# Every fourth leaky ReLU of the edge scores in two pieces, and the eigenvector parts in the first batches

## The chip, the cores and the metric

One core of a Trainium2 chip runs the whole program. The metric is the device time of one execution in microseconds (us). TensorE (PE in the rows, its weight loads PEld), VectorE (DVE), ScalarE (ACT), GpSimd (POOL) and SyncE (SP) run their own instruction streams and wait for each other on semaphores.

## What is computed

Four graph layers, each `x = layernorm(x + layer(x))`, on x of shape (128 graphs, 64 nodes, 256 features). Layers 0 and 1 (a graph network with windows of an LSTM, a graph convolution with batch norms) lie before the stage of this change. Layer 2 is the edge attention with four heads of 64 features and 512 edges, here cut to its scores:

```python
Xq = (H @ W_lin.T).reshape(bt, n, h, dh)
Qs = Xq[:, src]
Kt = Xq[:, dst]
e = jnp.einsum('behd,hd->beh', jax.nn.leaky_relu(Qs + Kt, 0.2), a)
e = e + jnp.log(A0[src, dst] + EPS)[None, :, None]
# softmax of e over the edges of one source node, then Y = sum of attn * Xv[dst], then Y @ W_out.T
```

Layer 3 needs the eigenvectors U of the normalised Laplacian of the adjacency matrix, and computes `U @ ((relu((U.T @ x) @ W1 + b1)) @ W2 + b2)`.

## The kernel before

The stage is in `edge_attention` (lines 1285 to 1492). The block before it ends with the queries of all graphs in SBUF (`xq`), rows of two graphs on 128 partitions. The stage runs over b = 0 to 127, one graph each, with 128 feature rows in each of C = 2 halves k and E = 512 edges:

- VectorE builds "stacks" (`build(dve, j)`, line 1359): for a batch j of four b it writes the queries of the four graphs as a high part (L1366) and a low part (L1368), four instructions a batch. There are three stacks; from j = 3 on a build waits until the gathers of batch j - 3 are done. Stacks 0 and 1 are built in the block before (`queries_ready`).
- TensorE gathers: for each b two matmuls (L1469) with a stack as weights and the 0/1 matrix `e_gather` as the moving operand give Qs + Kt of all 512 edges in PSUM, `ps_g[b % 3]`, 128x1024, one half k in each of two banks. Gather b waits until the leaky ReLU of b - 3 is done.
- ScalarE runs the leaky ReLU (L1340, Prelu) of both halves at once from `ps_g` into one of seven buffers `leaky`.
- TensorE multiplies with the vector a: `dots(r)` (L1454), eight matmuls for four b, which the profile shows as 16 records. It is issued after the gathers of b = 4r + 6, and waits for the leaky ReLU of 4r + 3.

After each 32 b (a quarter, eight batches) the scores of the quarter go through the softmax: `maximum` (L1381 to L1384), the exponential on ScalarE (L1335, after b % 32 == 12), `total` (L1388 to L1390), `inverse` in two halves (L1394), `weights` (L1397), then four transposes on TensorE (`turn`, L1461, after the gathers of b % 32 == 28), the copy of the high part on ScalarE (L1330, after b % 32 == 31) and the low part on VectorE (L1402). VectorE's order is written out by hand in `on_vector`: in batch j of the next quarter, `maximum` stands behind build j where j % 8 == 2, `total` where it is 4, the halves of `inverse` where it is 5 and 6.

VectorE also computes the eigenvectors for layer 3 in eight parts (`Eigenvectors.part`, lines 388 to 451). `EV_AT` (L1302) says behind which batch each part stands: batches 8 to 27. Part 3 ends with sums of squares, GpSimd makes inverse norms of them (`inverse_norm`, L382 to L386), and part 4 waits for these. The parts work in a part of `xq` whose queries are used up by batch 8 (L1300, `ev.place`). GpSimd's queue holds, behind the norm, six DMAs (L1323) that bring operands of the late values back from DRAM, two as each of three places in `xq` is used up (after stacks 11, 15 and 19). After b = 127 TensorE computes the late values (`LATER`), the last quarter goes through its softmax, and the attention begins; SyncE and GpSimd start its preparation when the last dot products are done.

Of the kernel before, what the change touches and what calls it, by code (L numbers as in the profile page):

```python
# [9 lines left out]
P = 128  # L10
# [479 lines left out]
def overlay(nc, name, shape, dt):  # L490


    with nc.sbuf_tensor(name, shape, dt) as t:
        return t
# [790 lines left out]
def edge_attention(nc, sem, c, m, ev, low, xq, acol, attn, hT, later):  # L1285
# [6 lines left out]
    with ExitStack() as ctx:  # L1292
# [4 lines left out]
        stack = [[sb(f"stack{i}{n}", [P, TWO, D], F32R) for n in range(2)] for i in range(STACKS)]  # L1297
        ps_g = [ctx.enter_context(nc.psum_tensor(f"sc_g{i}", [P, C, E], F32)) for i in range(GATHERS)]
        ps_s = [ctx.enter_context(nc.psum_tensor(f"sc_s{i}", [P, E], F32)) for i in range(2)]
        ev.place(xq[0:N, 6 * E:8 * E])  # L1300
        squares, norms = (sem("ev_" + n) for n in ("squares", "norms"))
        EV_AT = {8: 0, 11: 1, 15: 2, 16: 3, 19: 4, 23: 5, 24: 6, 27: 7}  # L1302
        score, top, tops, ex, run, tot = (xq[:, n * E:(n + 1) * E] for n in range(6))
        load, zero, placed, stacked, gathered, leaked, dotted, diff, exped, weighed, turned, high, low = (
            sem("sc_" + n) for n in ("load", "zero", "placed", "stack", "gathered", "leaky", "dot", "less_maximum",
# [3 lines left out]
        LATER = [GROUPS - 1] + list(range(later.FIRST, GROUPS - 1))  # L1309
        ps_v = [z[:, :, :].rearrange("p c (h d) -> p (c h) d", d=D) for z in ps_g]  # L1310
        BATCH = 2 * TWO
        COLUMN_HALVES = (slice(0, EC // 2), slice(EC // 2, EC))
        def on_sync(sp):
            sp.dma_start(ac[:, :], acol).then_inc(load, 16)
# [10 lines left out]
        def on_scalar(act, weights_ready):  # L1325
            a = nc.scalar

            def weights_hi(q, n=0, part=slice(0, EC)):
                act.wait_ge(turned, q + n + 1)
                a.activation(attn[0][:, part, q * P:(q + 1) * P], ps_s[(q + n) % 2][:, :].rearrange("p (k e) -> p k e", k=EC)[:, part],  # L1330
                             ACT.Copy).then_inc(high, 1)

            def exponent(q):
                act.wait_ge(diff, q + 1)
                a.activation(ex, top, ACT.Exp).then_inc(exped, 1)  # L1335
            for b in range(B):
                act.wait_ge(gathered, b + 1)
                if b >= RING:
                    act.wait_ge(dotted, (b - RING) // 4 + 1)
                a.activation(leaky[b % RING][:, :, :], ps_g[b % GATHERS][:, :, :], ACT.Prelu, alpha=SLOPE).then_inc(leaked, 1)  # L1340
                q, at = b // PER_Q - 1, b % PER_Q
                if q >= 0 and at == 12:
                    exponent(q)
                if q >= 0 and at == PER_Q - 1:
                    weights_hi(q)
            def values(n):
                act.wait_ge(valued, n + 1)
                a.activation(group_of(hT, LATER[n]).rearrange("p c (h d) -> p (c h) d", d=D), ps_v[n % GATHERS], ACT.Copy).then_inc(
                    values_copied, 1)
            values(0)  # L1350
            exponent(QUARTS - 1)
            weights_ready(act)
            values(1)
            values(2)
            for n, part in enumerate(COLUMN_HALVES):
                weights_hi(QUARTS - 1, n, part)
            values(3)

        def build(dve, j):
            if j >= STACKS:  # L1360
                dve.wait_ge(gathered, (j - STACKS + 1) * BATCH)
            for n in range(2):
                h, o = slice(n * N, (n + 1) * N), slice((1 - n) * N, (2 - n) * N)
                rows = xq[h, j * TWO * D:(j + 1) * TWO * D].rearrange("p (t d) -> p t d", d=D)
                hi, lo = stack[j % STACKS][n][h, :, :], stack[j % STACKS][n][o, :, :]
                nc.vector.tensor_copy(hi, rows).then_inc(stacked, 1)  # L1366
                dve.wait_ge(stacked, 4 * j + 2 * n + 1)
                nc.vector.tensor_tensor(lo, rows, hi.bitcast(F32), ALU.subtract).then_inc(stacked, 1)  # L1368
# [72 lines left out]
        def on_tensor(pe):  # L1441
            t = nc.tensor

            def dots(r):
                pe.wait_ge(leaked, 4 * r + 4)
                q, at = r // SLOTS, r % SLOTS
                if r == 0:
                    pe.wait_ge(placed, 2 * C)
                if at == 0 and q >= 2:
                    pe.wait_ge(high, q - 1)  # L1450
                    pe.wait_ge(low, q - 1)
                for k in range(C):
                    for j in range(4):
                        i = t.matmul(ps_s[q % 2][32 * j:32 * j + 32, :], apad[:, k, at * 32:at * 32 + 32], leaky[(4 * r + j) % RING][:, k],  # L1454
                                     start=at == 0 and k == 0, stop=at == SLOTS - 1 and k == C - 1, tile_position=(0, 32 * j))
                i.then_inc(dotted, 1)

            def turn(q, n=0, part=range(EC)):
                pe.wait_ge(weighed, q + n + 1)
                for k in part:  # L1460
                    i = t.transpose(ps_s[(q + n) % 2][:, k * P:(k + 1) * P], tops[:, k * P:(k + 1) * P], c["ident"][:, :])  # L1461
                i.then_inc(turned, 1)
            for b in range(B):
                if b % BATCH == 0:
                    pe.wait_ge(stacked, b + 4)
                if b >= GATHERS:
                    pe.wait_ge(leaked, b - GATHERS + 1)
                for k in range(C):
                    i = t.matmul(ps_g[b % GATHERS][:, k], stack[b // BATCH % STACKS][b % 2][:, b // 2 % TWO, k * P:(k + 1) * P],  # L1469
                                 m["gather"][:, :], start=True, stop=True)  # L1470
                i.then_inc(gathered, 1)
                if b % 4 == 2 and b > 4:
                    dots(b // 4 - 1)
                if b >= PER_Q and b % PER_Q == PER_Q - 4:
                    turn(b // PER_Q - 1)
            dots(B // 4 - 1)
            for n, g in enumerate(LATER):
                if n:
                    pe.wait_ge(rows_in[n - 1], 32)
                if n >= GATHERS:  # L1480
                    pe.wait_ge(values_copied, n - GATHERS + 1)
                hi, lo = later.rows(g)
                for r in range(TILES):
                    f = slice(r * P, (r + 1) * P)
                    for k in range(C):
                        i = product(t, ps_v[n % GATHERS][:, r], (hi[:, k, f], lo[:, k, f]), [z[:, k] for z in later.weights], k == 0, k == C - 1)
                i.then_inc(valued, 1)
            turn(QUARTS - 1, 0, range(EC // 2))
            turn(QUARTS - 1, 1, range(EC // 2, EC))
# [1190 lines left out]
def network(nc, a, out):  # L2680
# [14 lines left out]
    with ctx:  # L2695
# [10 lines left out]
        with ExitStack() as wide:  # L2706
            m, spectral, scores, place, later, hidB, layers = first_layers(nc, layer_sem, wide, c, bi, ev, hT, values, a, x1, x2, par1, par2)
            xq = hidB[:, :, :, :].rearrange("p g c n -> p (g c n)")
            res = overlay(nc, "attention_residual", [P, 2 * TILES * D], F32)
            with (nc.sbuf_tensor("attn_hi", [P, EC, QUARTS * P], F32R) as attn_hi,  # L2710
                  nc.sbuf_tensor("attn_lo", [P, EC, QUARTS * P], F32R) as attn_lo):
                attn = (attn_hi, attn_lo)
# [84 lines left out]
```

## Time and profile before

| | us |
|---|---|
| median of 3 timed runs | 1881.48 |
| lowest, highest | 1880.25, 1885.63 |
| profiled execution | 1882.7 |
| its span, first to last instruction | 1880.6 |
| TensorE busy in the span | 1802.4 |
| VectorE busy | 1458.5 |
| ScalarE busy | 1103.4 |
| GpSimd busy | 585.1 |
| mean granted TensorE clock, share of full speed | 0.986 |

The edge scores take from about 1483 to 1624 us of the span. A row of a group shows instructions of one line together: busy time, mean duration, the idle time of the engine before them, and what ended it. A timeline row shows where a run of the same instructions starts, how long the run is, and how many they are. An idle engine costs nothing unless the next one waits for it, so the chain of waits is read beside it.

### The profile page before, as it was taken

Reading aid. Unit: us, or ns where it says so; the run is one execution under the profiler, and the core shown is the slowest. Engines: PE = TensorE matmul, PEld = TensorE weight load, DVE = VectorE, ACT = ScalarE, POOL = GpSimd, SP = SyncE. Lnnn points to the kernel's source line nnn. Section 1 sums busy time; section 2 is a strip of 40 time slices with the busy share of each in tenths; the row PEclk is TensorE's granted clock in tenths of the full one; section 3 lists DMA queues with packets and bytes.
Section 4 is the critical chain, followed back from the end, with each engine's and each line's share of the span. In section 5 each row is a group of like instructions: output and inputs, shape, how many; then the busy total and the mean of one; then the engine's idle time right before and its main releaser. Section 6 shows DMA issues by size and latency. Waiting matters only on the chain. (4 is left out here: it accounts for less than half of the span.)

```text
span 1880.6 us, 35370 instructions
## 1 busy us (share of the span) xinstructions
PE 1802.4 (96%) x13191; PEld 1467.1 (78%) x13191; DVE 1458.5 (78%) x3920; ACT 1103.4 (59%) x1737; POOL 585.1 (31%) x1646
## 2 busy tenths in 40 slices
PE   7999999999999999999999999989799899999997
PEld 6777878888899999988887778867588534588875
DVE  7889876666576677878988879978667579798775
ACT  5555565445455455445344437757577688766676
POOL 3454421233323433000000015446544101104655
PEclk9999999999999999999999999999889999999999
DMA  4012010001000000010000034312222202003223
GB/s 138 26 35 69 2 40 6 1 1 45 1 1 1 1 1 1 1 46 1 1 1 1 1 96 136 102 45 90 67 79 70 100 1 68 12 1 103 81 77 106
DMA packets 63415, 77.75 MB, mean 41 GB/s; under 512 B 3974, under 2 KB 55436, under 8 KB 63244
## 3 DMA queue, kind: packets, MB, share of 16 engines
q1 hardware_dynamic: 62380, 72.35, 11.9%
q0 software_dynamic: 864, 3.15, 0.5%
q8 instruction: 104, 1.70, 0.4%
q14 instruction: 67, 0.55, 0.1%
HBM read 47.17 MB, written 28.31 MB: 40 GB/s over the span
## 5 line engine op out<-in xcount | busy, mean ns | idle before, releaser
L2123 ACT ACTIVATE l_gates<-l_acc,l_b 128x512 f32<-128x512 f32 (+1 forms) x408 | 240.3, 621 | 83.9 <-PE l_acc L480 82.1
L478 PE MATMUL l_acc<-l_x_hi,l_w1x_hi 128*128 128x336 f32 (+1 forms) x544 | 188.3, 346 | 1.1 <-ACT l_gates L2123 0.8
L480 PE MATMUL l_acc<-l_x_lo,l_w1x_hi 128*128 128x336 f32 (+1 forms) x544 | 187.6, 345 | 0.0
L479 PE MATMUL l_acc<-l_x_hi,l_w1x_lo 128*128 128x336 f32 (+1 forms) x544 | 187.2, 344 | 0.0
L478 PE MATMUL l_acc<-l_x_hi,l_w0x_hi 128*128 128x512 f32 x464 | 181.5, 391 | 3.4 <-ACT l_gates L2123 3.4
L2012 ACT ACTIVATE l_x_hi<-hT 128x512 fp32r<-128x512 f32 (+1 forms) x112 | 82.5, 787 | 173.1 <-PE l_acc L480 173.1
L479 PE MATMUL l_acc<-l_x_hi,l_w0x_lo 128*128 128x512 f32 x464 | 180.6, 389 | 0.0
L480 PE MATMUL l_acc<-l_x_lo,l_w0x_hi 128*128 128x512 f32 x464 | 180.6, 389 | 0.0
L2133 ACT ACTIVATE l_gates<-l_cell 128x512 f32<-128x512 f32 (+1 forms) x112 | 63.9, 571 | 168.9 <-DVE l_cell L2184 139.3
L249 POOL TENSOR_TENSOR bi_shifted<-bi_shifted 32x126 f32<-32x126 f32 (+61 forms) x62 | 18.1, 291 | 389.9 <-DVE bi_shifted L236 389.9
L1340 ACT ACTIVATE leaky<-sc_g 128x1024 f32<-128x1024 f32 x128 | 121.2, 1032 | 17.5 <-PE sc_g L1469 17.2
L478 PE MATMUL l_acc<-l_h_hi,l_w0h_hi 128*128 128x512 f32 x320 | 124.8, 390 | 0.7 <-DVE l_h_lo L2201 0.7
L2312 POOL TENSOR_TENSOR n_tmp<-n_stats 128x4 f32<-128x4 f32 x64 | 13.4, 209 | 358.3 <-DVE n_stats L2300 356.8
L480 PE MATMUL l_acc<-l_h_lo,l_w0h_hi 128*128 128x512 f32 x320 | 124.5, 389 | 0.0
L479 PE MATMUL l_acc<-l_h_hi,l_w0h_lo 128*128 128x512 f32 x320 | 124.5, 389 | 0.0
L478 PEld LDWEIGHTS l_acc<-l_x_hi,l_w1x_hi 128*128 128x128 f32 x544 | 102.3, 188 | 21.7 <-issue 11.4
L2329 ACT ACTIVATE hT<-hT,n_shift,n_rstd 128x256 f32<-128x256 f32 x192 | 100.0, 593 | 29.2 <-POOL n_shift L2324 29.2
L480 PEld LDWEIGHTS l_acc<-l_x_lo,l_w1x_hi 128*128 128x128 f32 x544 | 102.1, 188 | 8.6
L479 PEld LDWEIGHTS l_acc<-l_x_hi,l_w1x_lo 128*128 128x128 f32 x544 | 102.3, 188 | 8.0
L478 PEld LDWEIGHTS l_acc<-l_x_hi,l_w0x_hi 128*128 128x128 f32 x464 | 87.1, 188 | 23.6 <-ACT l_gates L2123 5.7
L2181 DVE TENSOR_TENSOR l_gates<-l_gates 128x512 f32<-128x512 f32 (+1 forms) x72 | 43.9, 609 | 75.8 <-ACT l_gates L2123 74.4
L480 PEld LDWEIGHTS l_acc<-l_x_lo,l_w0x_hi 128*128 128x128 f32 x464 | 87.1, 188 | 18.3
(519 smaller groups left out, 5345.0 us busy)
## 6 DMA issues: line engine op xcount, KB each, us to landing
xin<-in_x_t SPq DMA_DIRECT2D x16, 512.0 KB, 3.7
hidB<-in_x SPq DMA_DIRECT2D x16, 512.0 KB, 4.9
x<-hT SPq DMA_DIRECT2D x16, 512.0 KB, 3.2
hidB<-x SPq DMA_DIRECT2D x16, 512.0 KB, 3.8
x<-hidB SPq DMA_DIRECT2D x16, 512.0 KB, 2.9
attention_residual<-x SPq DMA_DIRECT2D x16, 512.0 KB, 3.8
out_x<-hT SPq DMA_DIRECT2D x16, 512.0 KB, 2.9
l_rawx<-in_wih SPq DMA_DIRECT2D x4, 1024.0 KB, 6.1
```

Of the source, the lines that this page charges most:

```text
L249: s.after(g.tensor_tensor(prod, vb[:, lo:].unsqueeze(1).to_broadcast([self.Q, 2, w]), self.p[k % 2][:, 2:4].unsqueeze(2).to_broadcast([sel ...
L478: t.matmul(out, left[0], right[0], start=start, stop=False)
L479: t.matmul(out, left[1], right[0], start=False, stop=False)
L480: return t.matmul(out, left[0], right[1], start=False, stop=stop)
L1340: a.activation(leaky[b % RING][:, :, :], ps_g[b % GATHERS][:, :, :], ACT.Prelu, alpha=SLOPE).then_inc(leaked, 1)
L2012: i = nc.scalar.activation(as_windows(xs[s % 2][0][:, ch, 0:bg * nw], nw), cols(p, bg, nw, group, k, ch), ACT.Copy)
L2123: i = a.activation(gates[:, j, q, 0:n], acc[:, j, q, 0:n], FUNC[q], bias=b[:, o:o + 1])
L2133: a.activation(tcell[:, j, 0:n], cell[:, j, 0:n], TANH).then_inc(tc, 1)
L2181: v.tensor_tensor(i_, i_, g_, ALU.mult)
L2312: s.add(p.tensor_tensor(apart, even[:, :, 1], odd[:, :, 1], ALU.subtract))
L2329: i = a.activation(rows[:, r, :], rows[:, r, :], ACT.Identity, bias=self.shift[:, g, r:r + 1], scale=self.rstd[:, g, r:r + 1])
```

## The change

The leaky ReLU of each b with b % 4 == 3 becomes two activations, one for each half k of 512 elements; the others stay whole. For this, both semaphores count halves: `gathered` rises by one for each of the two matmuls of a gather, `leaked` by one for each piece and by two for a whole leaky ReLU. The first piece waits for the first half of the gather alone, and the gather three b later waits half by half for the pieces. Where ScalarE also waits for a free `leaky` buffer, this wait now stands first. The eight eigenvector parts stand behind batches 1 to 8, so they can't use `xq` there, and get a place of 4 KB a partition at the address where `attention_residual`, and `attn_hi`, lie later.

```diff
-        ev.place(xq[0:N, 6 * E:8 * E])
-        EV_AT = {8: 0, 11: 1, 15: 2, 16: 3, 19: 4, 23: 5, 24: 6, 27: 7}
+        EV_AT = {1: 0, 2: 1, 3: 2, 4: 3, 5: 4, 6: 5, 7: 6, 8: 7}
+        FIRST = 3
             for b in range(B):
-                act.wait_ge(gathered, b + 1)
                 if b >= RING:
                     act.wait_ge(dotted, (b - RING) // 4 + 1)
-                a.activation(leaky[b % RING][:, :, :], ps_g[b % GATHERS][:, :, :], ACT.Prelu, alpha=SLOPE).then_inc(leaked, 1)
+                if b % 4 == FIRST:
+                    for k in range(C):
+                        act.wait_ge(gathered, C * b + k + 1)
+                        a.activation(leaky[b % RING][:, k], ps_g[b % GATHERS][:, k], ACT.Prelu, alpha=SLOPE).then_inc(leaked, 1)
+                else:
+                    act.wait_ge(gathered, C * b + C)
+                    a.activation(leaky[b % RING][:, :, :], ps_g[b % GATHERS][:, :, :], ACT.Prelu, alpha=SLOPE).then_inc(leaked, C)
         def build(dve, j):
             if j >= STACKS:
-                dve.wait_ge(gathered, (j - STACKS + 1) * BATCH)
+                dve.wait_ge(gathered, (j - STACKS + 1) * BATCH * C)
             def dots(r):
-                pe.wait_ge(leaked, 4 * r + 4)
+                pe.wait_ge(leaked, (4 * r + 4) * C)
-                if b >= GATHERS:
-                    pe.wait_ge(leaked, b - GATHERS + 1)
+                before = b - GATHERS
                 for k in range(C):
-                    i = t.matmul(ps_g[b % GATHERS][:, k], stack[b // BATCH % STACKS][b % 2][:, b // 2 % TWO, k * P:(k + 1) * P],
-                                 m["gather"][:, :], start=True, stop=True)
-                i.then_inc(gathered, 1)
-                if b % 4 == 2 and b > 4:
+                    if before >= 0:
+                        pe.wait_ge(leaked, C * before + (k + 1 if before % 4 == FIRST else C))
+                    t.matmul(ps_g[b % GATHERS][:, k], stack[b // BATCH % STACKS][b % 2][:, b // 2 % TWO, k * P:(k + 1) * P],
+                             m["gather"][:, :], start=True, stop=True).then_inc(gathered, 1)
+                if b % 4 == FIRST - 1 and b > 4:
                     dots(b // 4 - 1)
+            ev.place(overlay(nc, "ev_work", [N, 2 * E], F32)[:, :])
```

## Rows read from the trace of the kernel before

**Rows 1.** The page: the span, and the costliest groups' row of the leaky ReLU

```profile
span 1880.6 us, 35370 instructions
...
L1340 ACT ACTIVATE leaky<-sc_g 128x1024 f32<-128x1024 f32 x128 | 121.2, 1032 | 17.5 <-PE sc_g L1469 17.2
```

**Rows 2.** Busy time by stretch: PE, PEld, DVE, ACT, POOL, clock, DMA share, GB/s

```profile
1483.00:1518.00 35.00, 32.95 (x181) 14.14 (x181) 20.33 (x45) 30.36 (x33) 0.53 (x1) 1.00 0.00 1
...
1553.00:1588.00 35.00, 33.71 (x198) 14.57 (x197) 33.10 (x70) 31.28 (x35) 5.74 (x10) 1.00 0.28 91
```

**Rows 3.** Chain of waits, one round: start, us, what

```profile
1576.63 1.85 PE sc_s L1454 x16
```

**Rows 4.** Timeline of PE and ACT, one round: start, us, instructions, idle before

```profile
1574.82 3.77 ACT L1340 ACTIVATE leaky<-sc_g 128x1024 f32<-128x1024 f32 x4 [0.59 <-PE sc_g L1469]
1575.89 0.73 PE L1469 MATMUL sc_g<-e_gather,stack 128*128 128x512 f32 x2 [0.18 <-ACT leaky L1340]
1576.56 1.92 PE L1454 MATMUL sc_s<-leaky,apad 128*32 128x512 f32 x16
1578.41 1.67 PE L1469 MATMUL sc_g<-e_gather,stack 128*128 128x512 f32 x6
1579.18 3.77 ACT L1340 ACTIVATE leaky<-sc_g 128x1024 f32<-128x1024 f32 x4 [0.59 <-PE sc_g L1469]
```

**Rows 5.** Timeline of PE in narrow windows: single gather halves

```profile
1574.62 0.39 PE L1469 MATMUL sc_g<-e_gather,stack 128*128 128x512 f32 x1
...
1578.41 0.50 PE L1469 MATMUL sc_g<-e_gather,stack 128*128 128x512 f32 x1
```

**Rows 6.** Timeline of ACT: copies, and activations with scale and bias columns

```profile
1400.01 0.60 ACT L939 ACTIVATE hidB<-c_hid 128x512 f32<-128x512 f32 x1 [1.13 <-PE c_hid L480]
1400.51 0.59 ACT L940 ACTIVATE hT<-c_hid 128x512 f32<-128x512 f32 x1
1400.98 1.03 ACT L931 ACTIVATE x2t<-c_mix 128x1024 fp32r<-128x1024 f32 x1
1404.73 1.51 ACT L922 ACTIVATE oS<-hT,par 128x512 f32<-128x512 f32 x2
...
1553.91 0.59 ACT L1330 ACTIVATE attn_hi<-sc_s 128x512 fp32r<-128x512 f32 x1
1554.38 6.75 ACT L1340 ACTIVATE leaky<-sc_g 128x1024 f32<-128x1024 f32 x7
```

**Rows 7.** Timeline of ACT: table load, and the exponential of the third quarter

```profile
1531.88 1.28 ACT L1335 ACT_TABLE_LOAD   x1
...
1567.92 0.63 ACT L1335 ACTIVATE hidB<-hidB 128x512 f32<-128x512 f32 x1
1568.43 5.79 ACT L1340 ACTIVATE leaky<-sc_g 128x1024 f32<-128x1024 f32 x6
```

**Rows 8.** Timeline of DVE: the last instruction of stack 23

```profile
1582.33 0.69 DVE L1368 TENSOR_TENSOR stack<-hidB,stack 64x512 fp32r<-64x512 f32 x1
```

**Rows 9.** Timeline of DVE: part 1 and what follows it, part 3's ends

```profile
1526.73 0.21 DVE L401 TENSOR_REDUCE lam<-hidB 64x1 f32<-64x64 f32 x1
...
1527.96 0.42 DVE L1366 CAST stack<-hidB 64x512 fp32r<-64x512 f32 x1
...
1551.86 0.22 DVE L414 TENSOR_TENSOR hidB<-hidB 64x64 f32<-64x64 f32 x1
...
1553.60 0.14 DVE L422 COPY hidB<-hidB 32x1 f32<-32x1 f32 x1
```

**Rows 10.** Timeline of POOL: first and last instruction of the norm

```profile
1552.88 0.09 POOL L382 MEMSET ev_scalars<- 64x1 f32 x1 [68.56 <-DVE ev_scalars L417]
...
1555.07 0.48 POOL L386 TENSOR_SCALAR ev_scalars<-ev_scalars 64x1 f32<-64x1 f32 x1
```

**Rows 11.** Timeline of DVE in an early batch: the start of a stack

```profile
1494.97 0.42 DVE L1366 CAST stack<-hidB 64x512 fp32r<-64x512 f32 x1 [2.05 <-PE sc_g L1469]
```

**Rows 12.** Timeline of DVE: the last quarter's maximum

```profile
1625.91 0.69 DVE L1381 TENSOR_TENSOR hidB<-sc_s,e_log_adj 128x512 f32<-128x512 f32 x1 [0.83 <-PE sc_s L1454]
```

## The prediction

> **What bounds the kernel now.** First the page: the profiled execution took 1882.7 us, its span is 1880.6 us, and the median of the three timed runs is 1881.48 us [rows 1]. What lies around the span is 2.1 us, and I take it as unchanged. The change touches one stage alone, the edge scores, where 128 leaky ReLUs of 1.03 us run on ScalarE in 121.2 us, with 17.5 us of idle time before them, nearly all until a gather of TensorE ends [rows 1]. The table by stretches shows no engine full: of 35 us, TensorE is busy 33 to 34, ScalarE 30 to 31, VectorE 20 in the first quarter and 33 in the third, at a granted clock of 1.00 (2.4 GHz) [rows 2]. So it is a loop between two engines that bounds it, and the chain of waits and the timeline show it.
>
> The loop turns once in four b. ScalarE runs four leaky ReLUs in 3.77 us and stands 0.59 us; starts are 1579.18 - 1574.82 = 4.36 us apart [rows 4] (4.37 over the others). The link that closes it is the piece b % 4 == 3. Leaky ReLU 83 takes 1.03 us; 0.05 us later gather 86, which writes its buffer, starts (1575.89); 0.67 us later the dot products (1576.56); 1.85 us later gather 87 (1578.41); its two halves and the signal take 0.77 us until leaky ReLU 87 starts (1579.18) [rows 3, 4]. Sum 1.03 + 0.05 + 0.67 + 1.85 + 0.77 = 4.37. The other three leaky ReLUs have slack.
>
> **The split leaky ReLU.** It shortens two of these terms. Gather 86 no longer waits for the whole of 83: its second half waits for the second piece. And leaky ReLU 87 starts when the first half of gather 87 is there. The new loop, term by term:
> - The second piece starts one piece after the first and lasts a piece. No 128x512 Prelu out of sc_g is in the trace. The nearest are 128x512 copies out of PSUM: 0.59 or 0.60 us each, the next start 0.47 or 0.50 us later [rows 6]; a 128x1024 copy takes 1.03 us [rows 6], as the 128x1024 Prelu does, so the function costs nothing of its own. I take 0.49 + 0.59 = 1.08. The upper bound is a pair of 128x512 activations with scale and bias columns, 1.51 us together [rows 6]; the lower is 0.47 + 0.59 = 1.06.
> - Signal 0.05. The second half of the gather, begun from standstill, has its weights still to load: a first half takes 0.50 us where a following one takes 0.39 [rows 5], so 0.10; then 0.33 to the dot products (half of the 0.67, which hold one such load and two halves). Together 0.48.
> - Dot products 1.85, unchanged [rows 3].
> - The first half of gather 87 alone, 0.50 [rows 5], and 0.04 of signal.
>
> Sum 1.08 + 0.48 + 1.85 + 0.54 = 3.95 us, 0.42 less. ScalarE itself would need 3 x 0.905 (one start to the next, from 3.77 less 1.03 over three) + 0.98 = 3.70, TensorE 8 x 0.236 + 1.94 = 3.83 (dot products with 0.09 until they start); so the loop still decides, but with two engines close behind. From leaky ReLU 3 to 127 there are 31 rounds: 31 x 0.42 = 13.0 us.
>
> The added signal after each first half and wait before each second half aren't free a priori. Within the row of six gather halves the step is (1.67 - 0.39 - 0.10) / 5 = 0.236 us, signals and waits that are already met among them [rows 4, 5]. I take the new ones at nothing. A cost below nothing is excluded: nothing is taken away. Above, 0.05 us a round (1.6 us in all) is in the range. The Trainium skill, "TensorE: Matmul & The Clock Gate", section "The cost: per-tile semaphore tail", counts 26 ns for each matmul that signals where packed matmuls end together; two such signals lie on the loop, and an estimate by it would take 31 x 0.05 = 1.6 us of the gain. These gathers follow each other at 0.236 us, and no row here shows such a tail.
>
> **What the round gives back.** Five rounds hold other work of ScalarE. The one with the table load (1.28 us) and the first exponential [rows 7] is bound by ScalarE already and gains nothing: minus 0.47 (the 0.42, and 0.05 for the extra piece). The two further exponentials (0.52 until the next start) make the round 2.72 + 0.98 + 0.52 = 4.22, minus 0.27 each; the two copies of weights (0.47) [rows 6] 4.17, minus 0.22 each. Three rounds hold four transposes on TensorE (`turn`, about 0.44 us); before, TensorE's idle time hid them, now 0.3 us sticks out each: minus 0.9. The last leaky ReLU, in two pieces, ends 0.06 later. Sum 0.47 + 0.54 + 0.44 + 0.9 + 0.06 = 2.4.
>
> **VectorE is late next.** It builds the stacks that TensorE gathers from, in an order fixed by the program, and the softmax pieces stand between them. After the exponential of a quarter it makes the total, three stacks, two reciprocals and the weights. In the third quarter the exponential starts at 1567.92 [rows 7], and VectorE ends stack 23 at 1582.33 + 0.69 = 1583.02 [rows 8], 15.1 us after it; from the exponential's end on it has no idle stretch. TensorE wants that stack for gather 92, before at 1579.18 + 4.37 - 0.77 + 0.47 = 1583.25: met with 0.2 us to spare. After the change leaky ReLU 79 starts 0.52 + 2 x 0.905 = 2.33 us after the exponential, 91 three rounds of 3.95 later, and gather 92 is wanted 0.07 us ahead of that: 2.33 + 11.85 - 0.07 = 14.1 us. So TensorE waits 1.0 us once a quarter, and the loop, at standstill nowhere else, can't make it up: minus 3.0 us for three quarters.
>
> **The eigenvector parts.** The same eight pieces of VectorE move from batches 8 to 27 to batches 1 to 8; part 3, the longest, takes about 1.9 us, from 1551.86 to 1553.74, part 1, next to it, 1.2 us [rows 9]. They leave quarters in which VectorE has 2 us left and enter the one where it has 15 [rows 2], so I cost them at nothing. What hides them is VectorE's idle time of 2.05 us in each of those batches [rows 11]. A new batch is 3.95 us, a stack 2.35 (from 1494.97), which leaves 1.6 a batch, enough for all parts but part 3, which overdraws it once by 0.3, with over 1 us in hand since two stacks are built ahead. Part 4 waits for GpSimd's norm: from the squares' signal (1552.88) to its end (1555.07 + 0.48) 2.7 us [rows 10]; VectorE has the rest of part 3 (0.9) and stack 5 (2.35) in between, 3.3 us, so nothing waits. Were it late, stack 6 would be queued behind the wait and TensorE behind that. GpSimd's DMAs for the late values stand behind that norm in its queue and now start when stack 11 is done, earlier, with the same time to land. The other workspace costs nothing; attn_hi lies at the same place but is written from batch 15 on. Left where they were, the parts would cost up to their lengths in the full quarters; this is what their move buys, and it is no gain against before. A gain from it by itself is excluded: before, no round is longer for a late stack.
>
> **The sum.** 13.0 - 2.4 - 3.0 = 7.6 us. Behind the stage maximum, exponential, weights and the late values follow the last dot products (VectorE starts on them at 1625.91 [rows 12]), GpSimd and SyncE wait for the same signal, and all shifts as a whole. Profiled execution: 1882.7 - 7.6 = 1875.1; from the median, 1881.5 - 7.5 = 1874.0 us, 0.4% faster. About 0.3% (5.6 us) is what a measurement of this kernel can tell from no change, so the forecast lies near that edge.
>
> **Rivals.**
> - A, VectorE isn't late: the exponential comes earlier against TensorE than I put it, or a part that left gives its time back. Then 13.0 - 2.4 = 10.6 us: 1871. Against it: 15.1 us without a gap [rows 8].
> - B, the pieces are dear: at 1.51 us for two [rows 6] the loop is 4.38 us and nothing is gained; halfway, 3.8 us less VectorE's waits: 1878 to 1881.5. For it: there is no row for this very form. The Trainium skill, "ScalarE: Activation LUTs", section "Rules for kernel authors", gives 0.3 us an activation and 0.83 ns an element, 0.73 us for a piece: an estimate by it is a loop of 4.33 us, 1.2 us gained. The rows stand against it: 1.03 and 0.59 us for 1024 and 512 elements.
> - C, slower: the wait between the halves keeps the next weight load from running under the matmul. Each of the eight halves of a round would then show the 0.10 us of [rows 5]: 8 x 0.336 + 1.94 = 4.63 us, TensorE-bound, 31 x 0.26 = 8 us more: 1889.5. It decides from 0.07 us a half on. Against it: halves with a wait that is met follow at 0.236 us in [rows 4].
> - D, gained in the stage and lost behind it: a transfer or GpSimd that doesn't move along. All of them wait for the last dot products, so little speaks for it: 1877 to 1881.
>
> **Chances.** Forecast 0.58 (its own range 1872 to 1876.5, six sevenths of it beyond 0.3%), A 0.12, B 0.18, C 0.05, D 0.07. Faster by over 0.3%: 0.50 + 0.12 = 0.62; within it 0.08 + 0.18 + 0.07 = 0.33; slower 0.05. The range takes in A and most of B and D: 1870.5 to 1879.5.
>
> **What would show it.** In the timeline of the changed kernel: rounds of 3.95 us between first pieces, a second piece 0.49 us after the first, ScalarE idle about 0.25 a round; VectorE's idle time before stacks gone in the first quarter; three waits of TensorE for a stack, about 1 us each, at stacks 15, 23 and 31; ScalarE's stage 7 to 8 us shorter. Wrong if rounds are over 4.1 us (B), if gather halves step by over 0.3 us (C), if no wait for stacks is there (A), or if the first quarter is slower than the others' plain rounds (the parts cost).

## The result and the profile after

The changed kernel takes 1877.14 us (median of 16 runs, 1875.46 to 1880.44); the kernel before, run beside it, takes 1884.47 us (16 runs, 1879.78 to 1886.25). The ratio, which compares all the runs and not the two medians, is 0.9967, with a 95% interval of 0.9959 to 0.9975: 0.33% or 6.2 us faster (the medians are 7.3 us apart). The profiled execution took 1876.3 us, where 1875.1 was forecast (before 1882.7). Its page begins so (share of the span, number of instructions):

```profile
span 1874.2 us, 35407 instructions
...
PE 1799.0 (96%) x13191; PEld 1468.0 (78%) x13191; DVE 1459.6 (78%) x3920; ACT 1103.4 (59%) x1769; POOL 582.2 (31%) x1646
```

The busy times hardly move; the span is 6.3 us shorter than that of [rows 1]. The table by stretch says where that comes from (PE, PEld, DVE, ACT, POOL, clock, DMA share, GB/s; the first and third stretch answer to [rows 2], the second was not shown there):

```profile
1483.00:1518.00 35.00, 34.36 (x199) 15.46 (x199) 29.32 (x92) 33.52 (x44) 2.82 (x6) 1.00 0.01 1
1518.00:1553.00 35.00, 33.49 (x198) 14.70 (x196) 28.35 (x42) 32.77 (x44) 2.48 (x4) 1.00 0.18 61
1553.00:1588.00 35.00, 34.44 (x202) 15.30 (x200) 30.45 (x46) 32.78 (x46) 1.05 (x2) 1.00 0.09 31
```

In the first quarter VectorE now works 29.3 of 35 us instead of 20.3 (the eigenvector parts), ScalarE 33.5 instead of 30.4; in the third VectorE works 30.5 instead of 33.1. One round of ScalarE and TensorE, which answers to [rows 4] (timeline: start, length of the run, instructions, idle before):

```profile
1569.28 1.09 ACT L1342 ACTIVATE leaky<-sc_g 128x512 f32<-128x512 f32 x2 [0.19 <-PE sc_g L1475]
1570.25 2.87 ACT L1345 ACTIVATE leaky<-sc_g 128x1024 f32<-128x1024 f32 x3
1570.85 1.92 PE L1459 MATMUL sc_s<-leaky,apad 128*32 128x512 f32 x16
1572.70 1.11 PE L1475 MATMUL sc_g<-e_gather,stack 128*128 128x512 f32 x3
1573.29 0.60 ACT L1342 ACTIVATE leaky<-sc_g 128x512 f32<-128x512 f32 x1 [0.18 <-PE sc_g L1475]
```

Two pieces take 1.09 us, three whole leaky ReLUs 2.87, and the next first piece starts 1573.29 - 1569.28 = 4.01 us after this one (4.02 over the plain rounds, 4.37 before). ScalarE's idle time per round has fallen from 0.59 to 0.18 us.

The second thing to see is a quarter's last round, from leaky ReLU 91 to 95 (same view; VectorE's lines of `build` are L1371 and L1373 now, `total` begins at L1393, the transposes are L1466):

```profile
1562.89 0.64 ACT L1335 ACTIVATE hidB<-hidB 128x512 f32<-128x512 f32 x1
...
1563.56 1.23 DVE L1393 TENSOR_TENSOR_SCAN hidB<-e_keep_start,hidB 128x512 f32<-128x512 f32 x1 [1.75 <-ACT hidB L1335]
...
1577.31 0.69 DVE L1373 TENSOR_TENSOR stack<-hidB,stack 64x512 fp32r<-64x512 f32 x1
1577.35 1.09 ACT L1342 ACTIVATE leaky<-sc_g 128x512 f32<-128x512 f32 x2 [0.22 <-PE sc_g L1475]
1578.05 0.74 PE L1475 MATMUL sc_g<-e_gather,stack 128*128 128x512 f32 x2 [0.56 <-DVE stack L1373]
1578.63 0.60 PE L1466 MATMUL sc_s<-ident,hidB 128*128 128x128 f32 x4
1578.91 2.85 ACT L1345 ACTIVATE leaky<-sc_g 128x1024 f32<-128x1024 f32 x3 [0.47 <-PE sc_g L1475]
...
1582.55 0.60 ACT L1342 ACTIVATE leaky<-sc_g 128x512 f32<-128x512 f32 x1 [0.78 <-PE sc_g L1475]
```

The exponential starts at 1562.89, and VectorE ends stack 23, its answer to [rows 8], at 1577.31 + 0.69 = 1578.00: 15.1 us later, as before. TensorE stands for it until 1578.05, and this round takes 1582.55 - 1577.35 = 5.20 us; the two like it (from 59 and from 123 on) take 5.17 and 5.18. VectorE had itself stood 1.75 us just before, waiting for the exponential. The table of waits over the stage (waiter, what it waited for: us in all, times, longest) sums this up:

```profile
DVE hidB L1393 <- ACT hidB L1335: 7.4, 3, 4.0
...
PEld sc_g L1475 <- DVE stack L1373: 4.5, 9, 1.0
...
PE sc_g L1475 <- DVE stack L1373: 1.7, 3, 0.6
```

**Where the 6.3 us went.** From the start of leaky ReLU 3 to that of 127 the stage took 136.61 us before and takes 130.77: 5.84 less. What comes ahead of it ended 0.66 us earlier, and what follows took 0.18 longer (257.90 against 257.72). Neither of the two is the change's: the kernel before, profiled again, starts the stage 1.3 us earlier than the first time (`e10_before_again`, below).

### The profile page after: what moved, and what is told of

It is laid out like the page before. It is cut to its first block and busy times, and to the rows that moved or that the text cites. A ratio compares the mean times of both kernels' runs of the same rounds, so it can differ in the third digit from the quotient of the medians.

```text
span 1874.2 us, 35407 instructions
## 1 busy us (share of the span) xinstructions
PE 1799.0 (96%) x13191; PEld 1468.0 (78%) x13191; DVE 1459.6 (78%) x3920; ACT 1103.4 (59%) x1769; POOL 582.2 (31%) x1646
## 5 line engine op out<-in xcount | busy, mean ns | idle before, releaser
L479 PEld LDWEIGHTS l_acc<-l_x_hi,l_w0x_lo 128*128 128x128 f32 x464 | 87.4, 188 | 17.8
```

The source lines that it names most:

```text
L479: t.matmul(out, left[1], right[0], start=False, stop=False)
```

## The experiments

All edits are against the changed kernel, unless said otherwise. Each ratio is against executions of the kernel before that were made beside that run; their medians lie between 1881.4 and 1884.5 us. The stage is measured from leaky ReLU 7 to 127 (starts, 30 rounds), since the round from 3 to 7 depends on TensorE's clock in that execution, as the last section shows. "Turn" is a round that holds the transposes, three in all; they are within 0.03 us of each other but where two values stand.

| kernel | ratio to before (95%) | plain round | turn | 7 to 127 |
|---|---|---|---|---|
| before | 1 | 4.37 | 4.37 | 132.23 |
| before, again | 1.0007 (0.9994 to 1.0021) | 4.37 | 4.37 | 132.24 |
| changed | 0.9967 (0.9959 to 0.9975) | 4.02 | 5.18 | 126.72 |
| parts late | 0.9965 (0.9951 to 0.9980) | 4.02 | 5.18 | 127.60 |
| signals only | 0.9998 (0.9989 to 1.0008) | 4.45 | 4.45 | 134.59 |
| gather waits whole | 0.9988 (0.9975 to 1.0000) | 4.25 | 4.50 | 129.83 |
| start waits whole | 0.9996 (0.9986 to 1.0005) | 4.25 | 4.76 | 130.46 |
| all leaky ReLUs split | 0.9970 (0.9959 to 0.9981) | 4.02 | 5.11 | 127.27 |
| wait order | 0.9966 (0.9954 to 0.9979) | 3.96 | 5.18 | 125.73 |
| exponential early | 0.9945 (0.9929 to 0.9961) | 4.02 | 4.35 | 124.09 |
| the same, table first | 0.9944 (0.9928 to 0.9960) | 4.02 | 4.07, 4.35 | 122.70 |
| order and exponential | 0.9947 (0.9933 to 0.9961) | 3.96 | 4.35 | 122.74 |
| the same, with a table load that didn't take place | 0.9954 (0.9940 to 0.9969) | 3.96 | 4.35 | 122.75 |
| order, exponential, table | 0.9935 (0.9922 to 0.9948) | 3.96 | 4.35 | 121.31 |

### The eigenvector parts back where they were

```diff
-        EV_AT = {1: 0, 2: 1, 3: 2, 4: 3, 5: 4, 6: 5, 7: 6, 8: 7}
+        ev.place(xq[0:N, 6 * E:8 * E])
+        EV_AT = {8: 0, 11: 1, 15: 2, 16: 3, 19: 4, 23: 5, 24: 6, 27: 7}
...
-            ev.place(overlay(nc, "ev_work", [N, 2 * E], F32)[:, :])
```

> The split leaky ReLU as in the changed kernel, but the eight eigenvector parts where they were (batches 8 to 27, in their old place). Theory: the plain rounds stay at 4.02 us, since the loop decides them; what the move bought shows only where VectorE is late, about one more late stack near part 4 (batch 19 to 22, up to 1.2 us). From leaky ReLU 3 to 127: 132.0 us (changed kernel 130.8, before 136.6); ratio to the kernel before 0.9974. Rival 1, the parts take their whole 9 us from the three full quarters: 136 us or more, nothing gained over before. Rival 2, the move is worth nothing: 130.8 us, ratio 0.9967.

Measured: the stage (3 to 127) takes 131.63 us, against 130.77. The round from 83 on takes 4.73 us instead of 4.02, the one from 75 on 4.33 instead of 4.20, the one from 87 on 4.13 instead of 4.06, and the others are the same to 0.02. The table of waits has one more stand of TensorE's weight loads (L1374 is this kernel's L1373):

```profile
PEld sc_g L1476 <- DVE stack L1374: 5.9, 10, 1.0
```

So the move is worth 0.9 us in the stage, where VectorE is short of time, and the parts cost nothing in the first quarter. In the ratio this can't be told from nothing.

### Signals for halves alone

```diff
-                if b % 4 == FIRST:
+                if False:
...
-                        pe.wait_ge(leaked, C * before + (k + 1 if before % 4 == FIRST else C))
+                        pe.wait_ge(leaked, C * before + C)
```

Every leaky ReLU is whole again; each half of a gather still signals and waits.

> Each gather half signals and waits for itself and the eigenvector parts are early, but every leaky ReLU is whole and waits for both halves. Theory: the signals and waits cost nothing, and the parts' new place gives nothing by itself: plain rounds 4.37 us, 136.6 us from leaky ReLU 3 to 127, ratio 1.000. Rival, the signals are what made the measured round 0.07 us longer than forecast: rounds of 4.42 to 4.44, ratio 1.001, and the step between the gather halves over 0.24 us.

Measured: rounds of 4.45 us, where 4.37 was expected if signals and waits cost nothing. The timeline of TensorE and ScalarE says on which engine the 0.08 us lie:

```profile
1576.51 3.77 ACT L1345 ACTIVATE leaky<-sc_g 128x1024 f32<-128x1024 f32 x4 [0.68 <-PE sc_g L1475]
1580.96 1.02 ACT L1345 ACTIVATE leaky<-sc_g 128x1024 f32<-128x1024 f32 x1 [0.68 <-PE sc_g L1475]
...
1575.66 1.67 PE L1475 MATMUL sc_g<-e_gather,stack 128*128 128x512 f32 x6
1577.59 0.73 PE L1475 MATMUL sc_g<-e_gather,stack 128*128 128x512 f32 x2 [0.26 <-ACT leaky L1345]
1578.25 1.92 PE L1459 MATMUL sc_s<-leaky,apad 128*32 128x512 f32 x16
```

TensorE's rows are those of [rows 4] to the hundredth: six halves in 1.67, two in 0.73. The Trainium skill, "TensorE: Matmul & The Clock Gate", section "The cost: per-tile semaphore tail", counts 26 ns for each signal of matmuls that are packed into tiles of the array and end together. These gathers aren't packed, and for matmuls that follow each other, with a signal on every half, this run shows no such cost. ScalarE's four leaky ReLUs take 3.77 us as before, but stand 0.68 us instead of 0.59. The length alone would have favoured the rival; the rows clear the halves, and leave what changed on ScalarE: the order of its two waits, and that a whole leaky ReLU now raises `leaked` by two. The next run tests the first, on pieces that raise by one; the last section says what the rows tell of the second.

### The order of ScalarE's waits

```diff
-                if b >= RING:
-                    act.wait_ge(dotted, (b - RING) // 4 + 1)
                 if b % 4 == FIRST:
                     for k in range(C):
                         act.wait_ge(gathered, C * b + k + 1)
+                        if b >= RING and k == 0:
+                            act.wait_ge(dotted, (b - RING) // 4 + 1)
...
                 else:
                     act.wait_ge(gathered, C * b + C)
+                    if b >= RING:
+                        act.wait_ge(dotted, (b - RING) // 4 + 1)
```

Both waits stay; the one for the free buffer stands second again, as in the kernel before.

> The changed kernel with the two waits of a leaky ReLU in the order of the kernel before: first for the gather, then for the free buffer. In the run with signals alone the round was 4.45 instead of 4.37 us although TensorE's steps had not changed, and ScalarE ran a separate 38 ns wait instruction between the gather's end and the leaky ReLU. Theory, the swapped order costs 0.06 to 0.08 us a round: plain rounds 3.96 us, start of a first piece 0.04 us after the end of its gather half (changed kernel 0.10), 129.8 us from leaky ReLU 3 to 127, ratio 0.996. Rival, the signals of the first halves are what delays ScalarE: rounds stay 4.02, ratio 0.9967.

Measured: plain rounds of 3.96 us, and ScalarE's idle time before first pieces falls under what the view prints:

```profile
1571.21 1.08 ACT L1342 ACTIVATE leaky<-sc_g 128x512 f32<-128x512 f32 x2
1572.18 2.87 ACT L1347 ACTIVATE leaky<-sc_g 128x1024 f32<-128x1024 f32 x3
1575.17 1.08 ACT L1342 ACTIVATE leaky<-sc_g 128x512 f32<-128x512 f32 x2
1576.14 2.87 ACT L1347 ACTIVATE leaky<-sc_g 128x1024 f32<-128x1024 f32 x3
```

The wait written last becomes an instruction of its own in ScalarE's queue (ACTq), and the activation carries the other. The view by source line shows when it runs, first in the changed kernel, then in this one:

```profile
L1341 ACTq EVENT_SEMAPHORE  x31: 17/17/17, 1489.6 to 1616.3; - x31
```

```profile
L1341 ACTq EVENT_SEMAPHORE  x31: 17/17/17, 1491.9 to 1617.7; - x31
```

Though both are told at L1341, they are two waits. In the changed kernel it is that for the gather, and it runs at the last moment: in the round shown above the first half ends at 1573.20, the wait instruction starts at 1573.23 and lasts 17 ns, the activation starts at 1573.29, 96 ns after the half. With the order turned it is the wait for the buffer; it runs at 1574.765, long met, the half ends at 1575.13, and the activation starts at 1575.166, 37 ns after. The median over the stage is 97 ns in the changed kernel, 37 in the one before and here. So 0.06 us a round is the order of two lines. (In the kernel with signals alone it is 119 ns, and there the order is the smaller part, as the last section shows.)

Over 22 plain rounds 0.06 us would be 1.3, and the stage keeps 0.99: the rounds from 55, 87 and 119 on, next to the turns, grow from some 4.08 to 4.13, and the turns stay at 5.18. They wait for VectorE's stacks, and TensorE only comes to them earlier.

### The exponential four b earlier

```diff
-                if q >= 0 and at == 12:
+                if q >= 0 and at == 8:
```

> The changed kernel with the exponential of a quarter four leaky ReLUs earlier (after b % 32 == 8 instead of 12). VectorE stood 1.7 us ahead of each total, waiting for it (4.0 us for the first). Theory, TensorE waits for a stack because VectorE is late after the exponential: the three rounds with the transposes fall from 5.18 to about 4.4 us, the plain ones stay 4.02; 128.1 us from leaky ReLU 3 to 127, ratio 0.9954. Rival, those rounds are long by the transposes and the weights' way through three engines and not by a late stack: they stay at 5.2, ratio 0.9967.

Measured: 128.13 us from 3 to 127, turns of 4.35 us. VectorE's wait for the exponential is gone from the table, and of TensorE's stands for stacks one is left:

```profile
PEld sc_g L1475 <- DVE stack L1373: 1.3, 1, 1.3
```

The turn's round in ScalarE's timeline:

```profile
1576.77 1.09 ACT L1342 ACTIVATE leaky<-sc_g 128x512 f32<-128x512 f32 x2 [0.19 <-PE sc_g L1475]
1577.74 2.87 ACT L1345 ACTIVATE leaky<-sc_g 128x1024 f32<-128x1024 f32 x3
1581.12 1.09 ACT L1342 ACTIVATE leaky<-sc_g 128x512 f32<-128x512 f32 x2 [0.52 <-PE sc_g L1475]
```

So a turn's 5.18 us were 4.02, 0.33 for the transposes and 0.83 for the stack. This confirms the third term of the prediction, and that its cause is the exponential's place: VectorE stood idle for it, and only after it turned out late.

### The table load out of the stage

On top of the early exponential, a 64-element exponential ahead of the first leaky ReLU loads its table there:

```diff
+            a.activation(ev.scalars[:, 7:8], c["ones"][0:N, 0:1], ACT.Exp)
...
-                if q >= 0 and at == 12:
+                if q >= 0 and at == 8:
```

> As the one before, and ScalarE runs one exponential of 64 values ahead of the first leaky ReLU, where it stands about 2 us, so that the table load of 1.28 us falls there; its result is used nowhere. Theory: the table then in place serves both functions, the round of 5.6 us falls to 4.25, 126.8 us from leaky ReLU 3 to 127, ratio 0.9947. Rival, the table is loaded again at the exponential or at the leaky ReLU behind it: no gain over the run before, or 1.3 us lost at each switch.

Measured: the exponential's first round takes 4.21 us instead of 5.66, but the ratio doesn't move: 0.9944 after 0.9945. From 7 to 127 the gain is 1.39 us; leaky ReLU 3 starts 0.74 us later and the round after it took 4.33 instead of 4.04. The load ran from 1482.39 us on, beside the first gather (1482.43) and ahead of the first leaky ReLU; and TensorE's clock was at its lower level at the start of the stage in this execution. Most of the loss is the clock's: from the first gather to leaky ReLU 3 this kernel takes 4.21 us, four kernels with the same pieces at that level 4.02 or 4.03, and the one without the load, at full clock, 3.54. So the load in this place costs 0.2 us here, and what it would cost at full clock no trace shows. Nor could the ratio tell: 1.4 us are 0.07%, and its interval is 0.3% wide. (The first turn fell to 4.07 us with 4.30 in the round before it; the other two are 4.35.)

### Both orders and the table

The first attempt at all three put the short exponential outside ScalarE's part of the program:

> Waits in the order of the run before, the exponential after b % 32 == 8, and the unused exponential that brings the table moved to the end of ScalarE's work of the block before, where ScalarE stands 2.6 us. Theory, the three gains add up: plain rounds 3.96, no round over 4.4, 125.3 us from leaky ReLU 3 to 127 (before 136.6), ratio 0.994 or a little below. Rival, with rounds under 4 us VectorE is late again and the rounds with transposes return to 4.8 and over: 127 us or more.

Measured: plain rounds 3.96 us, turns 4.35, and the table load still in the first exponential's round (5.66 us): the third edit had no effect, and its exponential is nowhere in the trace. The ratio is 0.9954 (0.9940 to 0.9969), and from 3 to 127 the stage took 127.10 us where 125.3 was expected. It is a run of the other two, and so is the next one, which leaves the exponential out:

> The changed kernel with the waits of a leaky ReLU in their old order and the exponential after b % 32 == 8. Theory: plain rounds 3.96, those with transposes 4.35, the one with the table load 5.66; from leaky ReLU 7 to 127 122.9 us (changed kernel 126.7, before 132.2), so 3.8 us under the changed kernel; ratio 0.9945. Rival: with 3.96 us rounds VectorE is late again, rounds with transposes of 4.8 and over, 124 us or more.

Measured: 122.74 us from 7 to 127 (122.75 in the run before it). The two edits add up: 5.5 us for the change itself, 1.0 and 2.6 for them, 0.4 more when together, since VectorE no longer eats the order's gain. Then the short exponential at the end of ScalarE's work in the block before, inside its part:

```diff
                     def _(act):
                         layers[2](act)
+                        nc.scalar.activation(ev.scalars[:, 7:8], c["ones"][0:N, 0:1], ACT.Exp)
```

> The run before, and the unused exponential as the last thing that ScalarE does in the block before. In the earlier try it was laid out outside ScalarE's part of the block, and the table load stayed in the stage. Theory: ScalarE stands there 1 to 2 us until SyncE's last transfer has landed, the table load of 1.28 us falls into it, the round of 5.66 falls to 4.2: from leaky ReLU 7 to 127 121.5 us, the start of the stage 0.5 us later or less; ratio 0.994. Rival: the block's end waits for the table load, and what the round gains the start loses.

Measured: 1870.79 us, 0.9935 (0.9922 to 0.9948), the fastest of the study, 0.3% ahead of the changed kernel. From 7 to 127 it takes 1.43 us less than without the table; the ratios alone (0.9935 and 0.9947, with intervals that overlap) don't tell the two apart. ScalarE loads the table while it waits for the first gather anyway, and the first exponential's round is like the others:

```profile
1480.52 1.28 ACT L2734 ACT_TABLE_LOAD   x1
1481.82 0.20 ACT L2734 ACTIVATE ev_scalars<-ones 64x1 f32<-64x1 f32 x1
1483.60 2.86 ACT L1347 ACTIVATE leaky<-sc_g 128x1024 f32<-128x1024 f32 x3 [1.57 <-PE sc_g L1477]
...
1523.85 0.64 ACT L1335 ACTIVATE hidB<-hidB 128x512 f32<-128x512 f32 x1
1524.37 1.96 ACT L1347 ACTIVATE leaky<-sc_g 128x1024 f32<-128x1024 f32 x2
```

From the first gather to leaky ReLU 3 it takes 3.54 us, as the kernels at full clock without the load do. Whether the gather itself starts later for it, as the rival says, isn't shown: TensorE stood 3.34 us before it, and 2.9 to 3.5 in the other changed kernels.

### Each shortened link alone

The split shortens the loop at two places. One kernel takes back the first (the gather three b later waits for both pieces), one the second (the first piece waits for both halves):

```diff
-                        pe.wait_ge(leaked, C * before + (k + 1 if before % 4 == FIRST else C))
+                        pe.wait_ge(leaked, C * before + C)
```

> The changed kernel, but both halves of the gather three b later wait for both pieces; only the first piece's early start is left. By the theory's terms: 0.494 + 0.592 + 0.051 + 0.663 + 1.853 + 0.594 = 4.25 us a round, so the halved wait on TensorE is worth 0.23 of the 0.35 us. Rival, the early start is worth all: 4.02.

```diff
-                        act.wait_ge(gathered, C * b + k + 1)
+                        act.wait_ge(gathered, C * b + C)
```

> The changed kernel, but the first piece waits for both halves of its gather; only the halved wait on TensorE is left. By the theory's terms: 0.494 + 0.592 + 0.051 + 0.434 + 1.853 + 0.735 + 0.09 = 4.25 us a round. Rival, the loop is closed by the halved wait alone: 4.02.

Measured: plain rounds of 4.25 us in both, as expected of both. Each link is worth 4.25 - 4.02 = 0.23 us. From 4.45, where neither is shortened, either alone brings 0.20, since two pieces take 1.09 us where a whole leaky ReLU takes 1.03 and the first piece starts 0.02 sooner behind its gather (97 ns, not 119); the other on top of it brings its bare 0.23. So they add up along the loop. Alone, neither reaches the 0.3% that can be told from no change (0.9988 and 0.9996): a plain round is 0.12 us shorter than before, and 0.06 more go to the order of the waits.

### Every leaky ReLU in two pieces

```diff
-                if b % 4 == FIRST:
+                if True:
...
-                        pe.wait_ge(leaked, C * before + (k + 1 if before % 4 == FIRST else C))
+                        pe.wait_ge(leaked, C * before + k + 1)
```

> The changed kernel with all leaky ReLUs in two pieces and all gathers waiting half by half. Theory: only one link in four closes the loop, so the plain rounds stay at 4.02; ScalarE has 3 x 0.08 us more a round and the rounds with exponentials and copies grow by 0.24 (4.45 and 4.4): 131 to 131.5 us from leaky ReLU 3 to 127, no gain over the changed kernel. Rival: every split shortens the loop, rounds well under 4.0.

Measured: plain rounds of 4.02 us again, with 4 x 2 pieces. Where ScalarE has extra work it shows: 5.83 instead of 5.66 with the table load, 4.36 instead of 4.20 with an exponential, 4.32 instead of 4.16 with a copy of weights. The turn gains 0.07. In all 0.55 us more from 7 to 127. The loop goes through every fourth leaky ReLU, so splitting the other three buys nothing, and ScalarE pays about 0.05 us for each where it is the bound (0.08 was expected).

### The kernel before once more

> The kernel before, unchanged, for a second trace. TensorE stood 2.10 us between the last block and the first gather in the trace of before and 2.88 to 3.23 us in those of all the changed kernels, until SyncE's last transfer had landed. If that is chance of one execution, this trace shows about 2.9 as well; if it belongs to the change, about 2.1. The stage is 136.6 us from leaky ReLU 3 to 127 either way.

Measured: 1.0007 (0.9994 to 1.0021); the same rounds to 0.01 us, the stage 136.63 us (136.61). Its leaky ReLU 3 starts at 1484.94 us of the span, not 1486.23, and what follows the stage takes 256.36 us, not 257.72: the span is 2.6 us shorter with nothing changed. TensorE stands 3.00 us before the first gather, where it stood 2.10 the first time: the longer stand of the changed kernels (2.98 us in the first of them) is chance of an execution. So of two single profiles only the stage's own length may be compared, and the 0.66 us that the changed kernel is ahead at its start say nothing.

## Why the prediction was right

The forecast was 1874.0 us with a range of 1870.5 to 1879.5; measured were 1877.14. That is inside the range, but beyond the narrower one that the forecast gave to its own mechanism (1872 to 1876.5), so the number alone doesn't speak for it; the rounds do. The median of the kernel before is 1884.47 in these runs, 3.0 us above the one of three runs that the forecast was subtracted from, and this is nearly all of the 3.1 us. The medians themselves are 7.3 us apart where 7.5 was forecast, and that is luck: the stage gained 5.8 us and not 7.6, and the ratio says 6.2. As ratios, 0.9960 was forecast and 0.9967 (0.9959 to 0.9975) measured. One of the prediction's signs failed with it, a stage 7 to 8 us shorter.

**The pieces.** Right: 0.494 us from one start to the next and 0.592 for the second, 1.09 where 1.08 stood, read off copies of the same shape. The rival of dear pieces falls. By the estimate from the Trainium skill, "ScalarE: Activation LUTs", section "Rules for kernel authors", a piece would last 0.73 us, the trace has 0.598. That row of the section is for an activation whose bias is read from a [128,1] operand, and the leaky ReLU is called without one, so the estimate took it beyond what it states.

**The loop.** In the round from 23 on, and in the plain rounds of the first quarter alike, the terms are 1.085 for the pieces, 0.054 until the second half of the gather, 0.435 until the dot products, 1.854 for them, 0.496 for the first half of the next gather, and 0.096 until the first piece: 4.02. (In the round from 83 on TensorE comes 0.04 us late to the gather, since it stood for a stack before, and makes it up on the way to the dot products: 0.087 and 0.398.) The prediction had 1.08, 0.05, 0.43, 1.85, 0.50 and 0.04: 3.95. All but the last term are right to 0.01 us. **The term that was mis-sized is the signal ahead of the first piece, 0.04 against 0.096**, and the step that failed is "I take the new ones at nothing". The prediction looked for the price of new signals and waits on TensorE, and put a bound of 0.05 us a round on it in the range; it lay on ScalarE, where a wait that wasn't new only changed places with another. With the order turned back the rounds are 3.96. Over the 23 rounds that the sum took for plain it is 23 x 0.07 = 1.6 us; these rounds took 2.0 us more than put, and the turns 0.2 less, which together is the 1.8 that the sum was off. (The prediction works out ScalarE's step, 0.905 us, as 3.77 less 1.03 over three, which is 0.913; the trace has 0.904, so the slip is in the working alone.)

**What the round gives back.** Right to 0.02 us a round: 5.66 with the table load (5.65), 4.20 with an exponential (4.22), 4.16 with a copy (4.17), and 0.33 us a turn for the transposes (0.3).

**VectorE late.** Right in place, number and cause: three stands of TensorE, at stacks 15, 23 and 31, 15.1 us from exponential to stack. The size is 0.83 us a quarter, not 1.0: TensorE comes to the stack later than put, since its rounds are 4.02 us long and not 3.95. The early exponential takes exactly this away (5.18 to 4.35). Rival A said that VectorE isn't late; the kernel nearest to it, with exponential and waits in order, gains 132.23 - 122.74 = 9.5 us from 7 to 127, where A's sum over the same rounds is 30 x 0.42 - 2.4 = 10.2. The rest is small: 0.1 us a turn, 0.05 in each of the rounds behind a copy or an exponential (3.99 to 4.02 us, which the sum took for plain), 0.01 in the others.

**The eigenvector parts.** "At nothing" holds against before: the first quarter's rounds are 4.02 like all others, and VectorE's idle time before stacks, which is to hide the parts, falls from 12.1 us to 1.6 over the stage. That they would cost up to their lengths if left is too much: put back, they cost 0.9 us, since VectorE was idle 1.7 to 4.0 us a quarter for the exponential and took most of them there: from 1518 us on its busy time grows by 6.7 us, and those waits fall from 7.4 us to 3.1.

**The others.** Rival C, that a wait breaks the overlap of the weight loads, falls: TensorE's gather halves step at 0.23 to 0.24 us with a wait ahead of each. Rival D falls too: behind the stage 257.90 us against 257.72, within what two executions of one kernel differ by.

## What to carry to other kernels

Write a loop between two engines out as a chain of terms from the timeline before you shorten it; each term then predicts to hundredths of a microsecond, and only the instructions that close the chain are worth splitting. When one engine gets faster, look for the next to be late and ask what that one waits for: here VectorE stood idle for an exponential that sat four steps too late on ScalarE, and moving one line gave 2.6 us. And read a change of the order of waits as a change of the critical path: put the wait that ends last first, and look in the trace at which waits the closing instruction still carries itself.

## What the runs showed of the hardware

**Two waits ahead of an activation aren't alike.** With two `wait_ge` before one activation that raises its semaphore by one, the one written last runs as an instruction of its own. If it is the one that is met last, the activation starts 97 ns after the event, otherwise 37. By kernel the medians are 97 or 98 ns in the seven with the order of the change whose pieces raise by one, and 36 or 37 ns in the four with the order turned and in both profiles of the kernel before. It was seen on ScalarE for these two semaphores; other engines weren't tried.

**An activation that raises by two carries no wait.** In the kernel before a leaky ReLU raises `leaked` by one; a whole one now raises it by two, and all its waits stand in a separate instruction. The view by source line, first for the kernel with signals alone, then for the kernel before:

```profile
L1344 ACTq EVENT_SEMAPHORE  x128: 17/38/38, 1483.2 to 1625.4; - x128
```

```profile
L1339 ACTq EVENT_SEMAPHORE  x121: 17/17/17, 1490.0 to 1622.2; - x121
```

All 128 have one, of 38 ns where there are two waits; before, only the 121 with two waits had one, of 17 ns. Leaky ReLU 0 waits for its gather alone and starts 37 ns after it in the kernel before, 101 to 103 ns in ten kernels in which it raises by two. With two waits and the gather's last it is 118 or 119 ns (the kernel with signals alone, and leaky ReLU 92 of the changed kernel), with the gather's first 86 ns (leaky ReLU 92 of the wait order kernel). So of the 0.08 us a round that signals alone cost, some 0.05 go with the raise by two and 0.03 with the order. No run changes the raise by itself; this split is read from rows of kernels that differ in more.

**TensorE's clock at the start of the stage.** Before the first gather TensorE stands 2.1 to 3.5 us until the queries are in place. In some executions it is then granted its lower level, 1.2 GHz, in the first rounds, in others 2.4 GHz throughout. The table by stretch of the changed kernel, and of the one whose gather waits whole:

```profile
1476.00:1482.00 6.00, 3.06 (x26) 2.85 (x24) 3.41 (x7) 2.05 (x2) 0.00 (x0) 1.00 0.45 180
1482.00:1492.00 10.00, 9.33 (x46) 4.44 (x50) 7.62 (x27) 8.97 (x12) 0.53 (x1) 1.00 0.01 1
```

```profile
1476.00:1482.00 6.00, 4.73 (x40) 4.52 (x38) 4.87 (x9) 2.05 (x2) 0.00 (x0) 1.00 0.57 227
1482.00:1492.00 10.00, 8.26 (x31) 4.74 (x32) 6.02 (x22) 6.58 (x8) 0.53 (x1) 0.66 0.08 28
```

The mean granted clock of the second stretch is 1.00 in the one and 0.66 in the other. In the latter, leaky ReLU 3 started 4.02 us after the first gather (3.53 in the changed kernel), and the round from there took 4.54 us instead of 4.25: 0.8 us in all. The length of the stand doesn't explain it: 3.34 us in the fastest kernel left the clock up, 2.90 in the one with signals alone didn't. What decides it stays open. It adds to or takes from a single profile as much as some of these edits are worth, which is why the rounds are compared.

**One table for both functions.** The table that is loaded for the exponential serves the leaky ReLU as well: after it neither reloads. Its load is 1.28 us, and it costs the round that holds it 5.66 - 4.21 = 1.45 us.
